# Turning the next batch's normalised rows with a transposing load instead of PE transposes, in the first stage of a fused attention and expert kernel

## The reference, cut to what matters

```python
xn = _layernorm(x, axis=-1)                        # x: (8, 512, 512)
s = _L0_attn_ref(xn, Wq, Wk, Wv, Wo, Wg1, Wg2, norm_weight)
g = _silu(_L0_ffn_ref(xn, gate_w, Wg, Wu, Wd, sWg, sWu, sWd, shared_gate_w))
x = x + s * g
# inside _L0_attn_ref
q = silu(x @ Wq); k = silu(x @ Wk); v = x @ Wv     # then q and k are rotated
# per chunk: scores = q k^T * decay; o = scores v + (q * decay) S; S = lam * S + (k * decay)^T v
o = rmsnorm_per_head(o * sigmoid(x @ Wg1 @ Wg2)) * norm_weight
return o @ Wo
# inside _L0_ffn_ref
router_logits = flat @ gate_w.T                    # softmax, top 4, weights renormalised
```

## Time and profile before

| | |
|---|---|
| median of 3 runs | 1546.89 us |
| profiled execution | 1531.95 us |
| its span, first to last instruction | 1530.2 us |
| a turn of the first stage | 91.5 to 93.3 us, with the eighth to about 790 us |
| second stage | about 790 to 1284 us |
| third stage | about 1284 to 1530 us |

### The profile page before, as it was taken

How to read it: one execution, slowest core, us unless ns; L and a number is a source line. 1 busy time by engine, 2 the same in 40 slices (tenths; PEclk the granted TensorE clock), 3 DMA queues, 4 the chain that set the end, 5 groups by cost and what they waited for, 6 DMA issues and landing times.

```text
span 1530.2 us, 33035 instructions
## 1 busy us (share of the span) xinstructions
PE 1153.0 (75%) x9668; PEld 750.5 (49%) x9669; DVE 867.9 (57%) x1970; ACT 509.7 (33%) x977; POOL 705.6 (46%) x720
## 2 busy tenths in 40 slices
PE   2769789697997969879668776789898987354552
PEld 1345354554535445454536554566666665243431
DVE  6775858757596675958633444522121212477878
ACT  3324333242423424233224332344343433122221
POOL 2262543625345262443518999960000003587875
PEclk9989999898999989999878997899998988666655
DMA  6222212232132222311728876766666666999996
GB/s 236 97 116 97 119 60 91 103 117 110 48 123 99 87 110 79 126 69 61 263 68 202 220 199 171 199 163 162 169 165 165 168 164 197 226 279 289 317 307 235
DMA packets 286833, 239.94 MB, mean 157 GB/s; under 512 B 198256, under 2 KB 217840, under 8 KB 286672
## 3 DMA queue, kind: packets, MB, share of 16 engines
q1 hardware_dynamic: 262720, 160.61, 37.6%
q0 software_dynamic: 24080, 78.92, 15.6%
HBM read 92.66 MB, written 100.66 MB: 126 GB/s over the span
## 4 chain that ended last, share of the span: by engine, by line
PE 30%; issue 24%; DVE 18%; POOL 18%; DMA 5%; SPq 2%; ACT 1%; POOLq 1%; DVEq 1%; ACTq 0%
PE bank L459 23%; POOL expert_rows L709 8%; DVE qsin L1188 5%; DVE qswap L1185 3%; DMA s_x<-attention_out 3%; POOL stage L803 3%; PE bank L1691 2%; POOL we L760 2%; DVE probs L1283 2%; POOL wf L753 2%; PE bank L1684 2%; DVE acc L1479 1%; DMA xTc<-expert_rows 1%; PE bank L1674 1%; SPq L603 1%
## 5 line engine op out<-in xcount | busy, mean ns | idle before, releaser
L459 PE MATMUL bank<-xTc,we 128*128 128x128 f16 x4224 | 378.2, 248 | 80.9 <-issue 43.0
L459 PEld LDWEIGHTS bank<-xTc,we 128*128 (+1 forms) x4224 | 335.1, 112 | 171.3 <-issue 124.9
L803 POOL DMA_INDIRECT stage<-expert_outputs,idx x128 | 129.3, 1010 | 297.0 <-DVE idx L1470 261.6
L459 PE MATMUL bank<-we,h 128*128 (+1 forms) x528 | 173.2, 445 | 123.2 <-issue 78.3
L1449 DVE SCALAR_TENSOR_TENSOR hf<-bank,csc,sg 128x128 f32<-128x128 f32 x176 | 61.3, 348 | 301.4 <-ACT sg L1005 301.4
L702 POOL TENSOR_TENSOR qcos<-qs,tab 128x512 f32<-128x512 f32 x64 | 84.2, 1320 | 244.1 <-ACT qs L867 140.2
L1454 DVE TENSOR_TENSOR h<-hf,h 128x128 f16<-128x128 f32 x176 | 130.5, 741 | 67.9 <-ACT h L1012 67.9
L709 POOL DMA_INDIRECT expert_rows<-x,slots x128 | 124.1, 970 | 94.2 <-DVE slots L1256 53.9
L1005 ACT ACTIVATE sg<-bank,inv_x 128x128 f32<-128x128 f32 x176 | 64.5, 367 | 234.8 <-PE bank L459 234.8
L459 PEld LDWEIGHTS bank<-we,h 128*128 128x128 f16 x528 | 52.4, 106 | 163.1 <-issue 134.7
L1012 ACT ACTIVATE h<-hf 128x128 f16<-128x128 f32 x176 | 54.4, 309 | 228.2 <-DVE hf L1449 192.3
(11 more groups left out here) (169 smaller groups left out, 1675.2 us busy)
## 6 DMA issues: line engine op xcount, KB each, us to landing
expert_outputs<-y_sb SPq DMA_DIRECT2D x144, 256.0 KB, 2.3
x_t<-in_x_dram SPq DMA_DIRECT2D x32, 256.0 KB, 5.9
expert_rows<-x SPq DMA_DIRECT2D x32, 256.0 KB, 2.1
attention_out<-s_sb SPq DMA_DIRECT2D x32, 256.0 KB, 2.0
x_d<-in_x_dram SPq DMA_DIRECT2D x32, 256.0 KB
s_x<-attention_out SPq DMA_DIRECT2D x32, 256.0 KB
out_dram<-res SPq DMA_DIRECT2D x32, 256.0 KB, 5.5
stage<-in_w_gate_dram SPq DMA_DIRECT2D x18, 256.0 KB, 3.8
```

The costliest lines, as they stand in the source:

```text
L459: last = eng.matmul(dst, lhsT, rhs, start=(n == 0), stop=(n == len(pairs) - 1))
L803: pool.indirect_dma_start(out=ygat[:, k, n, :], out_offset=None, in_=yg, in_offset=bass.IndirectOffsetOnAxis(ap=idx[:, k, n:n + 1], axis=0 ...
```

## The change

The rows are turned by SP's transposing loads from the DRAM copy that `store_x` writes. The PE transposes, the ACT and DVE copies and their eight bank uses per turn are gone. `store_x` and the new `turn_x` stand together, ahead of chunk 1's output store in the loop and directly behind the weight loads ahead of it. `turn_x(0)` waits for the first three row stores to land, and `turn_x(3)` for the last. `small_products` moves behind `head_sums(3)` and `project_o(2)`, and `normalize(3)` and `high(3)` move from chunk 3 to the end of chunk 2.

```diff
@@ pass_a_order
-        if c == TPB - 1:
-            order += [("xh", 0), ("xl", 0), ("xh", 1), ("xl", 1)]
         if c > 1:
             order += [("wo", c - 2)]
-        if c == TPB - 1:
-            order += [("xh", 2), ("xl", 2), ("xh", 3), ("xl", 3)]
...
-    return order + [("small", 0), ("ms", TPB - 1), ("wo", TPB - 2), ("qk", 0), ...
+    return order + [("ms", TPB - 1), ("wo", TPB - 2), ("small", 0), ("qk", 0), ...
@@ SP
+            def turn_x(r, j):
+                if j == 0:
+                    wait(sp, "xrow_out", r, 16 * (TPB - 1))
+                    filled(sp, r, "v", TPB - 1, row=-1)
+                if j == TPB - 1:
+                    wait(sp, "xlast_out", r, 16)
+                apart(sp)
+                sp.dma_start_transpose(
+                    xT[:, :, :, j * P:(j + 1) * P].rearrange("p a c n -> p (a c) n"),
+                    xg[bass.ds(r[0] * SEQ + (E * REG + r[1] * SEQ + j * P), P), :]).then_inc(S("xT_ready"), 16)
+
+            def rows_and_columns(r):
+                for j in range(TPB):
+                    store_x(r, j)
+                for j in range(TPB):
+                    turn_x(r, j)
...
             sp.dma_start(raw_last[:, 2, :], w_down[E]).then_inc(last_in, 16)
+            rows_and_columns(FIRST)
             sp.wait_ge(const_pool, 3)
             sp.wait_ge(wlo_ready, 5)
             sp.wait_ge(whi_ready, 5)
-            for j in range(TPB):
-                store_x(FIRST, j)
...
-                    if c == 2 and not last:
-                        for j in range(TPB):
-                            store_x(following, j)
+                    if c == 1 and not last:
+                        rows_and_columns(following)
                     wait(sp, "s_ready", row, c + 1)
@@ ACT
-            def turn_high(r, j):
...
-                    if c == TPB - 1 and not last:
-                        turn_high(following, 0)
-                        high(following, 3)
-                        turn_high(following, 1)
...
                     if c == 2 and not last:
                         high(following, 2)
+                        high(following, 3)
@@ DVE
-            def turn_low(r, j):
...
-                        turn_low(following, 0)
-                        normalize(following, 3)
-                        for j in range(1, TPB):
-                            turn_low(following, j)
...
                     if c == 2 and not last:
                         normalize(following, 2)
+                        normalize(following, 3)
@@ PE
-            def rows_to_columns(turn, j):
...
-                wait(pe, "xTh_ready", (turn[0], turn[1] + 1), TPB)
-                wait(pe, "xTl_ready", (turn[0], turn[1] + 1), TPB)
+                wait(pe, "xT_ready", (turn[0], turn[1] + 1), 16 * TPB)
...
-                following(("small", 0))
                 head_sums(TPB - 1)
                 project_o(TPB - 2)
+                following(("small", 0))
                 following(("qk", 0))
```

More of the change, by code:

```diff
@@ L122, in pass_a_order @@
             order += [("kv", c)]
-    return order + [("small", 0), ("ms", TPB - 1), ("wo", TPB - 2), ("qk", 0), ("rb", TPB - 1), ("rt", 0),
+    return order + [("ms", TPB - 1), ("wo", TPB - 2), ("small", 0), ("qk", 0), ("rb", TPB - 1), ("rt", 0),
                     ("qk", 1), ("wo", TPB - 1)]
 def ahead(stage):
-    return int(stage[0] in ("xh", "xl", "small", "rt") or stage[0] == "qk" and stage[1] < 2)
+    return int(stage[0] in ("small", "rt") or stage[0] == "qk" and stage[1] < 2)
 def pass_a_banks():
@@ L484, in _ @@
         def _(sp):
-            credit(sp, [f"x_in{j}" for j in range(TPB)] + ["xrow_out", "s_out0", "s_out1", "raw_in"])
+            credit(sp, [f"x_in{j}" for j in range(TPB)] + ["xrow_out", "xlast_out", "xT_ready", "s_out0", "s_out1", "raw_in"])
             def load_x(r, j):
@@ L921, in finish @@
                                scale=ix(3)).then_inc(S("s_ready"), 1)
-            high((-1, 1), 0)
-            high((-1, 1), 1)
-            turn_high((-1, 1), 0)
-            high((-1, 1), 2)
-            turn_high((-1, 1), 1)
-            high((-1, 1), 3)
-            turn_high((-1, 1), 2)
-            turn_high((-1, 1), 3)
+            for j in range(TPB):
+                high((-1, 1), j)
             act.wait_ge(scale_ready, 1)
@@ L960, in turn_of_a @@
                 for c in range(1, TPB):
-                    if c == TPB - 1 and not last:
-                        turn_high(following, 0)
-                        high(following, 3)
-                        turn_high(following, 1)
                     if c > 1:
                         finish(row, c - 2)
-                    if c == TPB - 1 and not last:
-                        turn_high(following, 2)
-                        turn_high(following, 3)
                     roots(row, c - 1)
@@ L978, in turn_of_a @@
                         high(following, 2)
-                if not last:
-                    small_read(following)
+                        high(following, 3)
                 roots(row, TPB - 1)
@@ L983, in turn_of_a @@
                 finish(row, TPB - 2)
+                if not last:
+                    small_read(following)
                 high_o(row, TPB - 1)
@@ L1527, in pass_over @@
                         pe.sem_inc(S(f"bank{i}_full"), len(mine))
-            def rows_to_columns(turn, j):
-                for s, lo, ready in (("xh", 0, "xhi_ready"), ("xl", DM, "xlo_ready")):
-                    emptied(pe, turn, s, j)
-                    wait(pe, ready, (turn[0], turn[1] + 1), j + 1)
-                    for c in range(DC):
-                        last = pe.transpose(half(USE[s, j][0])[:, c * P:(c + 1) * P],
-                                            x16[:, j, lo + c * P:lo + (c + 1) * P], ident16)
-                    last.then_inc(full((s, j)), 1)
             def project_qk(turn, u):
```

46 lines of the change are left out of this document (9 added, 37 removed).

## The result

| | before | changed |
|---|---|---|
| median of 20 runs each, side by side on one chip | 1540.02 us | 1551.36 us |
| lowest to highest | 1522.52 to 1563.09 us | 1534.68 to 1570.36 us |
| profiled execution | 1531.95 us | 1546.65 us |
| its span | 1530.2 us | 1544.9 us |
| mean granted clock | 0.863 | 0.857 |

A forecast was written before the change was run, and what follows sets the result against it. No engine bounds the kernel everywhere; a turn shortens only as `spread(3)` comes earlier, with `small_products` set by PE or the loads. Start +7.9 us and seven turns -5.6 us gave +2.3 us on 1546.9, so 1549 us, range 1539 to 1566 us.

The forecast's parts named there:

- The start: Ahead of the loop: first small products wait for transposing loads queued behind SP's weight loads, 39.4 instead of 31.49, +7.9 us.
- PE's side of the tail: End of a turn: without transposes `head_sums(2)` starts 3.0 us earlier, and PE could start `small_products` at 499.5.
- The loads: End of a turn: four loads, issued every 1.27 us from 492.7, have data there at 500.0, which sets `small_products`.
- a sign of being wrong: In the loop: a transposing load landing later than 4 us after its issue would show the prediction wrong.
- The dear prices: Rival: four loads in a row choke, 1.67 us an issue and 5.6 us to land; +19.6 and +11.3 us, chance 0.22.
- Seven turns: 5.6 us off: Loop: q0 comes at 502.75 instead of 503.56, so each of seven turns is 0.8 us shorter.
- the clock rival: Loop: without transposes PE has more short gaps, five quick turns run at the lower clock; +8 us, 1557 us, chance 0.13.
- The sum: Whole kernel: +7.9 us at the start less 5.6 us in the loop gives +2.3 us, 1549 us.
- the signs of being wrong: Whole kernel: small products before 35, a load over 4 us, `project_o(1)` not a microsecond sooner, or unpriced later-stage moves.
- The range and the sign: Whole kernel: 1539 to 1566 us; chances 0.33 slower, 0.54 same, 0.13 faster by over 0.5%.
- "same": Whole kernel: a result within about 0.5%, 7.7 us, of the kernel before; chance 0.54.

The follow-up runs named there:

- a1_first_on_pe: Changed kernel with the first batch's rows turned by PE transposes as before, the loop keeping the loads; 1586.29 us, ratio 0.989 against the kernel before.
- a2_tables_behind: Changed kernel with the first batch's stores and loads issued ahead of the tables and last three weight loads; 1595.63 us, ratio 1.004 against the kernel before.
- a4_warm_gap: Changed kernel plus 24 extra matmuls a turn in chunk 1, where PE waits for `qd`; 1631.55 us, ratio 1.0214 against the kernel before.
- b4_warm_again: Changed kernel plus 24 extra matmuls a turn in chunk 1, repeated on another chip; 1626.96 us, ratio 1.0209 against the kernel before.
- c3: Changed kernel plus 32 extra matmuls a turn in chunk 0, ahead of output(0); 1631.34 us, ratio 1.0054 against the kernel before.
- c4: Changed kernel plus 32 extra matmuls a turn in chunk 0, and the first batch ahead of the tables; 1619.09 us, ratio 1.0136 against the kernel before.

## Why the prediction was right and where it was wrong

**The start: +7.9 us forecast, +7.1 us measured.** Right in mechanism and nearly in size. The stores were issued at 23.84, behind the weight loads as said, and the loads at 30.85 (forecast 32.15); four issues took 5.43 us and the last landing 3.6 us. `a1_first_on_pe` and `a2_tables_behind` show that SP's queue is what costs.

**PE's side of the tail: right.** `project_o(1)` was to start 2.3 us ahead of the third `low`'s end (488.0 against 490.29), and starts 496.53 against 498.84, so 2.3 us. `project_o(2)` was to start 6.5 us behind it and starts 6.3 us behind.

**The loads: right in place, 0.2 to 0.3 us dear.** First issue 2.4 us behind `low(2)`, as said; 1.34 us from one issue to the next for 1.27; landing 3.6 us in the median for 3.2 to 3.4. The small products start 9.9 to 10.0 us behind `low(2)`, for 9.7 forecast, and wait for the DMA in the turns at full clock (0.91 us in the row shown, for 0.3 to 0.8); the fourth load lands 9.9 us behind it, for 9.3 to 9.5. Two of the loop's seven groups had a load that landed later than 4 us (up to 4.8 us in the first turn, 4.1 us in the last), which I had named as a sign of being wrong. The dear prices of the earlier trace rows did not come.

**"Seven turns: 5.6 us off": this is the step that failed.** Six turns gave 0.6 us, and the first turn was 1.5 us longer instead (99.98 for 98.53; its tail gave nothing, 13.4 us for 13.3, with a load that landed 4.8 us after its issue). I had taken the turn to be as much shorter as q0 comes earlier behind `low(2)`, with everything ahead of `low(2)` as before. It wasn't: the stretch from chunk 1's state products to `low(2)` is 0.4 to 1.1 us longer, with PE at 1.2 GHz for longer, and `project_o(2)` fell at the lower clock in two turns of six. This is the clock rival, in a milder form than I had priced it (+8 us): no turn changed from the short kind to one 1.6 us longer, but all of them gave back about what the tail had gained. That the stretch is longer by its matmuls at the lower clock is read from the same matmuls in both kernels, and `a4_warm_gap` and `b4_warm_again` have it at 18.3 us without the lower clock. What is not shown is why the lower level lasts longer with the change, and that a whole turn gets shorter once it is gone: the kernels that were to show this (a4, b4, c3, c4) ran into another stall, and their turns got longer.

**The sum: +2.3 us forecast.** The first stage ended up 7.2 us longer in the profiled pair (7.1 + 1.5 - 0.6 = 8.0 up to the last q0, the rest in the eighth turn). The other 4 us of the 11.3 us between the medians lie in stages that no edit touches: in the profiles at hand the second stage takes from 485 to 512 us and the third from 234 to 258 us, in whatever kernel, and in this pair they were 6 us shorter and 14 us longer. I can't attribute them; that something unpriced moves a later stage was among the signs of being wrong. The means of the twenty runs differ by 12.3 us with a standard error of 3.6 us, which does not exclude a true difference of 7 us; the interval of the ratio, 9 to 21 us, just does, and it excludes the 2.3 us forecast.

**The range and the sign.** Slower by over 0.5% had a chance of 0.33 and happened; "same", with 0.54, did not. That the measured 1551 us lies so close to the 1549 us forecast is luck: the baseline fell by 7 us as the difference rose by 9. On another chip the same pair came out the other way, by 0.7% with an interval that just clears 1.

No kernel was found that clearly beats both. The changed kernel with the first batch turned by PE is the best candidate that ran (0.989, with an interval that just reaches 1).

## What to carry to other kernels

When a transpose goes from PE to a transposing load, ask first what stands ahead of its store in the queue: here the loop paid nothing, and the one batch ahead of the loop paid 7 us for weights that nobody needed yet. A gain read at the end of a turn is only a gain if the rest of the turn keeps its durations; where PE sits idle and comes back at 1.2 GHz (here for 3.8 us in one kernel and 6.4 us in the other), compare the same product's duration in both kernels before adding the gain up. And measure a pair on more than one chip before giving a change of under one per cent a sign.

## What the hardware showed that I had not expected

- One kernel, on three of four chips, takes 60 to 70 us more (1605 to 1610 us for 1540), 66 us of the 76 between two profiled executions in the first stage: during 16 back-to-back scatters PE, DVE and ACT start instructions late whose inputs are ready (ACT 17.4 us, "remote"). 12.4 us become 24.4 to 26.7 us per turn, at the same traffic.
- The granted clock and the matmul durations agree in time: in the changed kernel the clock is 0.50 from 474 to 484 us, the slow matmuls stand at 477.8 to 484.2, and those from 484.22 on run at full speed. So the clock of a short stretch tells which products run slow.
- Transposing loads of 256 KB issued four in a row hold SP's queue for 1.34 us each and land after 3.6 us in the median, 0.4 us more than the 80 single ones of the earlier trace rows.
